# Quantizing the hidden activations of a dense layer: the multiply and rounding on ScalarE, the bound and the cast on VectorE

## The chip, the cores and the metric

One core of one Trainium2 chip runs the whole program. The metric is the device time of one launch in microseconds (us), the median over several launches. Engines are named as the profile names them: PE is TensorE (PEld its weight loads), DVE is VectorE, ACT is ScalarE, POOL is GpSimd, and SP is the engine whose queue issues most of the DMAs.

## What is computed

The input is 4096 tokens of 512 values. The first half of the reference adds a pooled attention term and normalizes (`y` below), then runs a feed-forward layer whose operands are quantized to small integers; the second half (a causal convolution and a mixture of eight experts, two per token) follows it and is not touched. The part that matters:

```python
def activation_quant(x):
    scale = 127.0 / clip(max(abs(x), axis=-1), EPS, None)
    return clip(round(x * scale), -128, 127) / scale
def bitlinear(x, w):            # w is rounded to -1, 0, 1 times one scale
    xn = rmsnorm(x)
    return activation_quant(xn) @ weight_quant(w).T
h = silu(bitlinear(y, w1)) * bitlinear(y, w2)      # 2048 values per token
x = x + bitlinear(h, w3)
```

The integers -128 to 127 are exact in bf16, so the three products run as bf16 matmuls and the scales are applied behind them.

## The kernel before

The dense layer takes the 4096 tokens in 32 tiles of 128, one token per partition. Every engine has an instruction stream of its own, written by hand, and all five streams are generated by one loop, `pipeline`, over stages s; in one stage the streams work on different tiles, and semaphores tie them together. An engine executes its stream strictly in order, and so does the SP queue: a wait holds up everything behind it.

In stage s:

- **PE** multiplies tile s with w1 and w2, each in two halves of 1024 columns: w1 half 0 (L1429), w2 half 0 (L1441), w1 half 1 (L1429), w2 half 1 (L1441), eight matmuls each; then the 16 matmuls of tile s-2 with w3 (`down`, L1452). The w1 products share one PSUM area, so each half of w1 waits for ACT's silu of the half before. The first half waits for the transposed tile `QyT` (semaphore `qyt_in`), `down` for the transposed halves `QT` (`qt_in`).
- **ACT** takes silu of half 0 (L812), casts the rounded y of tile s+1 to bf16 (L803, `cast_y`), casts half 0 of the rounded hidden tile s-1 from int16 to bf16 (L818, `cast_h`), takes silu of half 1, casts half 1 of tile s-1, and squares the halves of tile s for their mean (L826), with one square of y (L798) between.
- **DVE** adds the output of tile s-3 (L1093, `x1_add`), takes the statistics of tile s+3 and centres it (L1033, L1035, L1041), takes the largest y of tile s+2 (L1056), quantizes the hidden tile s-1 (L1085, `h_quant`: all 2048 columns times the scale, bounded by 127, written as int16), multiplies half 0 of tile s with its silu and takes its largest value (L1071, L1077), finishes the norm of tile s+3 (L1048), does the same two steps for half 1, and quantizes y of tile s+2 (L1063, `y_quant`).
- **POOL** works out the scale of hidden tile s-1 (`h_scales`, L667 to L677, the last of which signals `hq_done`), the scales of y (L624 to L660), and adds the attention term to tile s+4 (L618).
- **SP** issues, in this order: the transposing DMA of y of tile s+1 (L450, `turn_y`), the store of an output tile (L424), the two transposing DMAs of hidden tile s-1 (L458, `turn_h`, one per half; each waits for its half of `qh_done`), and then loads and fills for later: the attention rows every second stage (`PJ`, L420), a piece of the convolution's taps and a small fill of the scratch (stages 6 to 21, L482 and L473), an input tile (`XR`, stages 7 to 26, L432), and the convolution's input in four DMAs (`XW`, stages 4 to 19, L440 and L442). Behind them comes `turn_y` of the next stage.

`Ih` (int16) and `Qh` (bf16) are one place in SBUF with two names, single-buffered; `QT` and `H` are double-buffered. The part of SP's stream that sets the order:

```python
if tile(s + 1):
    turn_y(s + 1)
if tile(s - 3):
    store_x1(s - 3)
if tile(s - 1):
    turn_h(s - 1, 0)
    turn_h(s - 1, 1)
if s % TB == 0 and TB < (s + 6) // TB < B:
    load_pj((s + 6) // TB)
```

In stage 32, the first without a new tile for PE, SP first issues 16 DMAs of XW (it waits for the last w2 products), then `turn_h` of tile 31. PE there runs `down(30)`, a first piece of the convolution (L1480), and `down(31)`.

Of the kernel before, what the change touches and what calls it, by code (L numbers as in the profile page):

```python
# [20 lines left out]
ALU = mybir.AluOpType  # L21
ACT = mybir.ActivationFunctionType
# [5 lines left out]
QMAX = 127.0  # L28
# [4 lines left out]
def adaln_ffn_moe(nc, x, cond, taps, rms_w, WkT, WoT, gamma, beta, w1T, w2T, w3T, Wr, We, be, out):  # L33
    B, S, D = x.shape
    FF = w1T.shape[1]
# [36 lines left out]
    with ctx:  # L72
        def sem(name):
            return ctx.enter_context(nc.semaphore(name))
# [13 lines left out]
        def place(name, at, shape, dt=F32):  # L88
            n = 4 if dt in (F32, F32R) else 2
            size = n  # L90
            for s in shape[1:]:
                size *= s
            assert at >= 0 and at + size // 4 <= words, (name, at, size, words)
            return nc.alloc_sbuf_tensor_at(name, list(shape), dt, offset=base + 4 * at)
# [14 lines left out]
        H = [place(f"H{i}", a_h + FF * i, [P, FF]) for i in range(2)]  # L109
        a = a_h + 2 * FF  # L110
        Ih = place("Ih", a, [P, FF], I16)
        Qh = place("Qh", a, [P, FF], BF16)
# [50 lines left out]
        def col(i):  # L163
            return [sm[:, 2 * i + t:2 * i + t + 1] for t in range(2)]

        YMS, YR, YM, YB, YI, YQ, OG = (col(i) for i in range(7))
        HR, HM, HB, HI, HQ, RSTD = (col(8 + i) for i in range(6))
# [11 lines left out]
        NH = 2  # L179
# [118 lines left out]
        qt_in = [[sem(f"qt_in{h}{t}") for t in range(2)] for h in range(2)]  # L298
        pool_a = sem("pool_a")
        g_done, u_done, silu_done, hm_done = (sem(n) for n in ("g_done", "u_done", "silu_done", "hm_done"))  # L300
        hsq_done, hq_done = sem("hsq_done"), sem("hq_done")
        pool_h = sem("pool_h")
        hmc_done = sem("hmc_done")
        hint_done, qh_done, down_done, x1_done = (sem(n) for n in ("hint_done", "qh_done", "down_done", "x1_done"))
# [28 lines left out]
        def tile(n):  # L333

            return 0 <= n < NT
# [427 lines left out]
        def _(act):  # L763
# [28 lines left out]
            def square_y(n):  # L792
                act.wait_ge(y_done, n + 1)
                if n:
                    act.wait_ge(ysq_done, n)
                if n >= 2:
                    act.wait_ge(yq_done, n - 1)
                nc.scalar.activation(JUNK, Y[n % 3][:], ACT.Square, scale=D ** -0.5,  # L798
                                     accum_out=YMS[n % 2]).then_inc(ysq_done, 1)

            def cast_y(n):
                act.wait_ge(yint_done, n + 1)
                nc.scalar.copy(Qy[n % 2][:], Iy[n % 2][:]).then_inc(yqt_done, 1)  # L803

            def silu(n, c):
                p = NH * n + c
                act.wait_ge(g_done, p + 1)
                if c == 0:
                    act.wait_ge(og_done, n + 1)
                if n:  # L810
                    act.wait_ge(hsq_done, p - 1)
                nc.scalar.activation(SG[c][:], GP.rearrange("p a c -> p (a c)"), ACT.Silu, scale=OG[n % 2]).then_inc(silu_done, 1)  # L812

            def cast_h(n, h):

                half = slice(FF // 2 * h, FF // 2 * h + FF // 2)
                act.wait_ge(hint_done, n + 1)
                nc.scalar.copy(Qh[:, half], Ih[:, half]).then_inc(qh_done, 1)  # L818

            def square_h(n, c):  # L820

                half = slice(FF // 2 * c, FF // 2 * c + FF // 2)
                act.wait_ge(hm_done, NH * n + c + 1)
                if n >= 2:
                    act.wait_ge(hq_done, n - 1)
                nc.scalar.activation(SG[c][:], H[n % 2][:, half], ACT.Square, scale=FF ** -0.5,  # L826
                                     accum_out=(HSB if c else HSA)[n % 2]).then_inc(hsq_done, 1)

            def halo(j):

                act.wait_ge(x1_done, KEEP)
                rows = XW[QD * j:QD * j + OB].rearrange("p (b c) i -> p b c i", c=CB)[:, 0:B // 2, 0, :]
                none = IDF[QD * j:QD * j + OB, :].rearrange("p (o i) -> p o i", o=1).broadcast_to([OB, B // 2, NI])
                nc.scalar.activation(rows, none, ACT.Copy, scale=0.0).then_inc(halo_done, 1)

            def stage(s):
                if s <= 0:
                    return
                if tile(s):
                    silu(s, 0)  # L840
                if s == 1:
                    square_y(3)
                elif tile(s + 1):
                    cast_y(s + 1)
                if tile(s - 1):
                    cast_h(s - 1, 0)
                if tile(s):
                    silu(s, 1)
                if tile(s - 1):
                    cast_h(s - 1, 1)  # L850
                if tile(s):
                    square_h(s, 0)
                if tile(s + 3):
                    square_y(s + 3)
                if tile(s):
                    square_h(s, 1)
                if 0 <= s - KEEP - 4 < NQ:
                    halo(s - KEEP - 4)
# [13 lines left out]
            square_h(0, 0)  # L872
            square_h(0, 1)
            pipeline(stage)


# [68 lines left out]
        def _(dve):  # L945
# [81 lines left out]
            def stats(n):  # L1027
                t = n % 2
                if n < TB:
                    dve.wait_ge(add_sum, n + 1)  # L1030
                else:
                    dve.wait_ge(sum_done, n + 1 - TB)
                nc.vector.bn_stats(BS[t], Y[n % 3][:]).then_inc(stats_done, 1)  # L1033
                dve.wait_ge(stats_done, n + 1)
                nc.vector.bn_aggr(MV[t], BS[t]).then_inc(mv_done, 1)  # L1035

            def center(n):
                t = n % 2
                dve.wait_ge(norm_in, 32)
                dve.wait_ge(mv_done, n + 1)  # L1040
                nc.vector.scalar_tensor_tensor(out=Y[n % 3][:], in0=Y[n % 3][:], scalar=MV[t][:, 0:1], in1=GAM[:],  # L1041
                                               op0=ALU.subtract, op1=ALU.mult).then_inc(gam_done, 1)
# [8 lines left out]
            def y_max(n):  # L1051
                t = n % 2
                dve.wait_ge(y_done, n + 1)
                if n >= 2:
                    dve.wait_ge(yq_done, n - 1)
                nc.vector.tensor_reduce(YM[t], Y[n % 3][:], AX.X, ALU.max, apply_absolute_value=True).then_inc(ymax_done, 1)  # L1056
# [17 lines left out]
            def h_max(n, c):  # L1074
                half = slice(FF // 2 * c, FF // 2 * c + FF // 2)
                dve.wait_ge(hm_done, NH * n + c + 1)
                nc.vector.tensor_reduce(HMC[n % 2][:, c:c + 1], H[n % 2][:, half], AX.X, ALU.max,  # L1077
                                        apply_absolute_value=True).then_inc(hmc_done, 1)

            def h_quant(n):  # L1080
                dve.wait_ge(hq_done, n + 1)
                if n:
                    for h in range(2):
                        dve.wait_ge(qt_in[h][(n - 1) % 2], 16 * ((n - 1) // 2 + 1))
                nc.vector.tensor_scalar(Ih[:], H[n % 2][:], HQ[n % 2], QMAX, ALU.mult, ALU.min).then_inc(hint_done, 1)  # L1085

            def x1_add(n):
                t = n % 2
                dve.wait_ge(down_done, n + 1)
                dve.wait_ge(od_done, n + 1)  # L1090
                if n >= 2:
                    dve.wait_ge(x1_out[t], 16 * (n // 2))
                nc.vector.scalar_tensor_tensor(out=X1[t][:], in0=DN, scalar=OD[n % 3], in1=xt(n),  # L1093
                                               op0=ALU.mult, op1=ALU.add).then_inc(x1_done, 1)
# [3 lines left out]
            def stage(s):  # L1098
                if s <= 0:
                    return  # L1100
                if tile(s - 3):
                    x1_add(s - 3)
                if tile(s + 3):
                    stats(s + 3)
                    center(s + 3)
                if tile(s + 2):
                    y_max(s + 2)
                if tile(s - 1):
                    h_quant(s - 1)
                if tile(s):  # L1110
                    h_mul(s, 0)
                    h_max(s, 0)
                for w, c in WORK.get(s, ()):
                    ternary(w, c)
                if tile(s + 3):
                    norm(s + 3)
                if tile(s):
                    h_mul(s, 1)
                    h_max(s, 1)
                if tile(s + 2):  # L1120
                    y_quant(s + 2)
                if s in (NT, NT + 1):
                    spread(s - NT)
# [150 lines left out]
            for q in range(NK // CC):  # L1274
                h = q % 2
# [338 lines left out]
```

## Time and profile before

| | us |
|---|---|
| median of 3 runs | 845.53 (844.99 to 846.36) |
| the profiled execution, its own time | 845.81 |
| its span, first to last instruction | 844.1 |
| PE busy | 740.7 (88%) |
| DVE busy | 564.4 (67%) |
| POOL busy | 477.3 (57%) |
| ACT busy | 396.8 (47%) |

The dense layer's pipeline fills most of the stretch from about 70 to 432 us of the span. The rows in the section after next come from the trace of this execution. A row of the timeline has the start, the duration, the engine, the line and what it writes and reads; xN means that N like instructions in a row are shown as one, from the start of the first to the end of the last; the bracket is the idle time before and what ended it. SPq is the issue of a DMA by SP. A DMA's landing is the time from its issue to its semaphore. All numbers of a row that is a group are totals and means.

### The profile page before, as it was taken

Reading aid. Unit: us, or ns where it says so; the run is one execution under the profiler, and the core shown is the slowest. Engines: PE = TensorE matmul, PEld = TensorE weight load, DVE = VectorE, ACT = ScalarE, POOL = GpSimd, SP = SyncE. Lnnn points to the kernel's source line nnn. Section 1 sums busy time; section 2 is a strip of 40 time slices with the busy share of each in tenths; the row PEclk is TensorE's granted clock in tenths of the full one; section 3 lists DMA queues with packets and bytes.
Section 4 is the critical chain, followed back from the end, with each engine's and each line's share of the span. In section 5 each row is a group of like instructions: output and inputs, shape, how many; then the busy total and the mean of one; then the engine's idle time right before and its main releaser. Section 6 shows DMA issues by size and latency. Waiting matters only on the chain.

```text
span 844.1 us, 12610 instructions
## 1 busy us (share of the span) xinstructions
PE 740.7 (88%) x3913; PEld 432.6 (51%) x3945; DVE 564.4 (67%) x831; ACT 396.8 (47%) x635; POOL 477.3 (57%) x738
## 2 busy tenths in 40 slices
PE   1745599999999999999989999657999999899994
PEld 0112244444444444444446653345788888778773
DVE  2469999999999999997734424397834654444442
ACT  2056466666768877776412524034322333333332
POOL 1037889888888888884200000003567766876864
PEclk9987899999999999999999999768999999999998
DMA  9984148899999985555698999986468778877876
GB/s 359 388 328 134 31 88 149 137 182 180 178 180 189 183 157 132 117 116 92 138 232 148 113 116 258 116 197 215 77 126 165 143 136 160 152 146 143 167 143 105
DMA packets 230270, 137.50 MB, mean 163 GB/s; under 512 B 162798, under 2 KB 195054, under 8 KB 229054
## 3 DMA queue, kind: packets, MB, share of 16 engines
q1 hardware_dynamic: 210094, 99.94, 59.0%
q0 software_dynamic: 15456, 36.47, 23.2%
q10 hardware_dynamic: 4656, 0.30, 0.5%
q8 instruction: 33, 0.54, 0.3%
q14 instruction: 31, 0.25, 0.1%
HBM read 80.27 MB, written 35.42 MB: 137 GB/s over the span
## 4 chain that ended last, share of the span: by engine, by line
PE 45%; DMA 13%; POOL 11%; DVE 11%; issue 9%; SPq 6%; ACT 4%; POOLq 0%; DVEq 0%; ACTq 0%
DMA out_x<-YS,IDS 8%; PE PS L1480 8%; PE PS L1452 7%; PE PS L1572 7%; PE PS L1429 7%; PE PS L1441 7%; PE PS L1507 4%; POOL out_x L751 3%; SPq L381 2%; POOL ZR L742 2%; DVE Ih L1085 2%; PE PS L1529 1%; DMA QyT<-Qy 1%; ACT Qh L818 1%; DMA QT<-Qh 1%
## 5 line engine op out<-in xcount | busy, mean ns | idle before, releaser
L1572 PE MATMUL PS<-W,ZH 128*128 x552 | 179.5, 406 | 8.2 <-DVE ZL L1339 6.1
L742 POOL DMA_INDIRECT ZR<-z_scratch,IDG x69 | 69.6, 1008 | 156.1 <-DVE IDS L1303 135.4
L1429 PE MATMUL PS<-W,QyT 128*128 128x512 bf16 x502 | 123.0, 387 | 26.8 <-DMA QyT<-Qy 15.2
L751 POOL DMA_INDIRECT out_x<-YS,IDS x69 | 110.8, 1606 | 59.1 <-SPq L560 29.7
L939 ACT ACTIVATE YS<-YS,SG 128x512 f32<-128x512 f32 x69 | 50.0, 724 | 159.9 <-DVE YS L1357 159.9
L1441 PE MATMUL PS<-W,QyT 128*128 128x512 bf16 x504 | 120.9, 381 | 0.4
L1452 PE MATMUL PS<-W,QT 128*128 128x512 bf16 x498 | 116.4, 383 | 4.4 <-DMA QT<-Qh 2.9
L1572 PEld LDWEIGHTS PS<-W,ZH 128*128 128x128 f32 x552 | 100.4, 191 | 29.7 <-issue 11.5
L1572 PE MATMUL PS<-W,ZL 128*128 x276 | 109.6, 397 | 0.0
L1339 DVE TENSOR_TENSOR ZL<-PS,ZH 128x512 fp32r<-128x512 f32 x69 | 47.7, 691 | 78.2 <-ACT ZH L928 78.2
L1429 PEld LDWEIGHTS PS<-W,QyT 128*128 128x128 bf16 x512 | 49.7, 99 | 90.0 <-DMA QyT<-Qy 17.3
L812 ACT ACTIVATE SG<-PS,sm 128x1024 f32<-128x1024 f32 x64 | 71.0, 1109 | 45.5 <-PE PS L1429 45.5
L818 ACT CAST Qh<-Ih 128x1024 bf16<-128x1024 int16 x64 | 66.4, 1040 | 52.5 <-DVE Ih L1085 52.5
L1452 PEld LDWEIGHTS PS<-W,QT 128*128 128x128 bf16 x512 | 50.4, 99 | 65.7 <-issue 5.5
L1441 PEld LDWEIGHTS PS<-W,QyT 128*128 128x128 bf16 x512 | 50.4, 98 | 61.5 <-issue 2.1
L1071 DVE TENSOR_TENSOR H<-SG,PS 128x1024 f32<-128x1024 f32 x64 | 77.7, 1214 | 3.4 <-PE PS L1441 3.1
L1357 DVE TENSOR_TENSOR YS<-PS,BEB 128x512 f32<-128x512 f32 x69 | 47.6, 690 | 48.0 <-DMA out_x<-YS,IDS 26.0
L1077 DVE TENSOR_REDUCE sm<-H 128x1 f32<-128x1024 f32 x64 | 78.1, 1220 | 2.2
L1480 PE MATMUL PS<-XW,BD 128*64 128x128 f32 x512 | 74.2, 477 | 0.3 <-DVE BD L1135 0.3
L826 ACT ACTIVATE SG<-H 128x1024 f32<-128x1024 f32 x64 | 67.2, 1050 | 0.7 <-DVE H L1071 0.7
L1480 PEld LDWEIGHTS PS<-XW,BD 128*64 128x64 f32 x512 | 47.9, 165 | 26.4 <-issue 1.2
L1572 PEld LDWEIGHTS PS<-W,ZL 128*128 128x128 f32 x276 | 52.4, 190 | 11.7
(217 smaller groups left out, 1059.8 us busy)
## 6 DMA issues: line engine op xcount, KB each, us to landing
XW<-out_x SPq DMA_DIRECT2D x64, 240.0 KB, 4.5
X<-in_x SPq DMA_DIRECT2D x32, 256.0 KB, 10.0
out_x<-X SPq DMA_DIRECT2D x32, 256.0 KB, 3.6
z_scratch<-ZZ SPq DMA_DIRECT2D x8, 1024.0 KB, 24.1
WRAW<-in_We SPq DMA_DIRECT2D x8, 1024.0 KB, 12.6
XR<-in_x SPq DMA_DIRECT2D x20, 256.0 KB, 4.1
stage<-in_w1T SPq DMA_DIRECT2D x4, 1024.0 KB, 8.0
stage<-in_w2T SPq DMA_DIRECT2D x4, 1024.0 KB, 11.9
```

Source lines behind the costliest of these rows:

```text
L742: pool.indirect_dma_start(ZR[m % UZ][:], None, z_d, bass.IndirectOffsetOnAxis(IDG[:, m:m + 1].bitcast(U32), 0)) \
L751: pool.indirect_dma_start(x1_d, bass.IndirectOffsetOnAxis(IDS[:, m:m + 1].bitcast(U32), 0), YS[m % UN][:], None, compute_op=ALU.add).then_ ...
L812: nc.scalar.activation(SG[c][:], GP.rearrange("p a c -> p (a c)"), ACT.Silu, scale=OG[n % 2]).then_inc(silu_done, 1)
L818: nc.scalar.copy(Qh[:, half], Ih[:, half]).then_inc(qh_done, 1)
L826: nc.scalar.activation(SG[c][:], H[n % 2][:, half], ACT.Square, scale=FF ** -0.5, accum_out=(HSB if c else HSA)[n % 2]).then_inc(hsq_done, 1)
L1071: nc.vector.tensor_tensor(H[n % 2][:, half], SG[c][:], UP[c].rearrange("p a c -> p (a c)"), ALU.mult) \
L1077: nc.vector.tensor_reduce(HMC[n % 2][:, c:c + 1], H[n % 2][:, half], AX.X, ALU.max, apply_absolute_value=True).then_inc(hmc_done, 1)
L1429: i = nc.tensor.matmul(GP[:, a, :], QyT[t][:, k, :], W12[:, k, o:o + CH], start=(k == 0), stop=(k == KD - 1))
L1441: i = nc.tensor.matmul(UP[c][:, a, :], QyT[t][:, k, :], W12[:, k, o:o + CH], start=(k == 0), stop=(k == KD - 1))
L1452: i = nc.tensor.matmul(DN, QT[t][:, k, :], W3[:, k, :], start=(k == 0), stop=(k == KF - 1))
L1480: i = nc.tensor.matmul(PS[P // 2 * u:P // 2 * u + P // 2, b % 8, HB2 * (q % 4):HB2 * (q % 4) + HB2], BD[c % 2][:, u, q, :], XW[:, HB2 * h: ...
L1572: x = nc.tensor.matmul(bank[i], zz[i % 2][:, k, :], W2[:, bass.ds(q, 1), part, k, :].rearrange("p o d -> p (o d)"), start=(k == 0 and n == ...
```

## The change

The hidden tile's quantization is cut at another place. ScalarE now multiplies by the scale and rounds to int16, reading H, in two halves (`quant_h`), where it had cast int16 to bf16. VectorE, which had multiplied, bounded and rounded all 2048 columns at once, now bounds by 127 and casts int16 to bf16 in place, in two halves (`cast_h`). Each half is placed in VectorE's stream behind the product and the maximum of the same half of tile s; `turn_h` on SP waits for `qh_done` as before, which VectorE now signals.

```diff
-            def cast_h(n, h):
+            def quant_h(n, h):
                 half = slice(FF // 2 * h, FF // 2 * h + FF // 2)
-                act.wait_ge(hint_done, n + 1)
-                nc.scalar.copy(Qh[:, half], Ih[:, half]).then_inc(qh_done, 1)
+                act.wait_ge(hq_done, n + 1)
+                if n:
+                    act.wait_ge(qt_in[h][(n - 1) % 2], 16 * ((n - 1) // 2 + 1))
+                nc.scalar.activation(Ih[:, half], H[n % 2][:, half], ACT.Copy, scale=HQ[n % 2]).then_inc(hint_done, 1)
...
                 if tile(s - 1):
-                    cast_h(s - 1, 0)
+                    quant_h(s - 1, 0)
                 if tile(s):
                     silu(s, 1)
                 if tile(s - 1):
-                    cast_h(s - 1, 1)
+                    quant_h(s - 1, 1)
...
-            def h_quant(n):
-                dve.wait_ge(hq_done, n + 1)
-                if n:
-                    for h in range(2):
-                        dve.wait_ge(qt_in[h][(n - 1) % 2], 16 * ((n - 1) // 2 + 1))
-                nc.vector.tensor_scalar(Ih[:], H[n % 2][:], HQ[n % 2], QMAX, ALU.mult, ALU.min).then_inc(hint_done, 1)
+            def cast_h(n, h):
+                half = slice(FF // 2 * h, FF // 2 * h + FF // 2)
+                dve.wait_ge(hint_done, NH * n + h + 1)
+                nc.vector.tensor_scalar(Qh[:, half], Ih[:, half], QMAX, None, ALU.min).then_inc(qh_done, 1)
...
                 if tile(s + 2):
                     y_max(s + 2)
-                if tile(s - 1):
-                    h_quant(s - 1)
                 if tile(s):
                     h_mul(s, 0)
                     h_max(s, 0)
+                if tile(s - 1):
+                    cast_h(s - 1, 0)
                 for w, c in WORK.get(s, ()):
                     ternary(w, c)
                 if tile(s + 3):
                     norm(s + 3)
                 if tile(s):
                     h_mul(s, 1)
                     h_max(s, 1)
+                if tile(s - 1):
+                    cast_h(s - 1, 1)
                 if tile(s + 2):
                     y_quant(s + 2)
```

## Rows read from the trace of the kernel before

**Rows 1.** Busy time (x instructions), granted clock, DMA share in one stretch of the layer.

```profile
core 0: us, PE busy (x) PEld busy (x) DVE busy (x) ACT busy (x) POOL busy (x), PEclk, DMA share, GB/s
300.00:400.00 100.00, 99.53 (x456) 45.34 (x464) 90.95 (x109) 69.19 (x102) 78.93 (x165) 1.00 0.56 118
```

**Rows 2.** Timeline, PEld: the first weight loads of tiles 6, 8, 20 and 22.

```profile
141.08 0.96 PEld L1429 LDWEIGHTS PS<-W,QyT 128*128 128x128 bf16 x5
...
163.16 0.77 PEld L1429 LDWEIGHTS PS<-W,QyT 128*128 128x128 bf16 x5 [0.31 <-DMA QyT<-Qy]
...
289.58 0.31 PEld L1429 LDWEIGHTS PS<-W,QyT 128*128 128x128 bf16 x2
...
310.30 0.75 PEld L1429 LDWEIGHTS PS<-W,QyT 128*128 128x128 bf16 x4
```

**Rows 3.** Chain that ended last, stages 10 and 16: start, duration, what.

```profile
193.59 1.48 SPq L458
...
201.04 5.46 DMA QyT<-Qy
...
256.57 1.71 SPq L458
...
263.85 5.17 DMA QyT<-Qy
```

**Rows 4.** Timeline of SP, stage 12, from the second hidden transposition to turn_y.

```profile
214.58 1.62 SPq L458 DMA_TRANSPOSE QT<-Qh  x1
...
218.04 1.88 SPq L432 DMA_DIRECT2D XR<-in_x  x1
...
222.01 2.46 SPq L450 DMA_TRANSPOSE QyT<-Qy  x1
```

**Rows 5.** Tile QyT, 155 to 290 us: who waited (us, times), and landings.

```profile
  PEld PS L1429: 4.1, 6
...
DMA to landing us min/median/max: 3.9/4.9/5.5
```

**Rows 6.** Groups: what is removed, and the rows nearest to what is added.

```profile
L812 ACT ACTIVATE SG<-PS,sm 128x1024 f32<-128x1024 f32 x64 | 71.0, 1109 | 45.5 <-PE PS L1429 45.5
L818 ACT CAST Qh<-Ih 128x1024 bf16<-128x1024 int16 x64 | 66.4, 1040 | 52.5 <-DVE Ih L1085 52.5
L1085 DVE TENSOR_SCALAR Ih<-H,sm 128x2048 int16<-128x2048 f32 x32 | 41.0, 1282 | 8.0 <-POOL sm L677 7.6 <-DMA QT<-Qh 0.3
...
L979 DVE TENSOR_SCALAR W<-TMP x12: 694/694/716, 26.7 to 98.6; 128x2048 bf16<-128x2048 int16 x12
```

**Rows 7.** Timeline, stage 31 and the start of 32: the hand-over to SP and the tail.

```profile
403.54 1.61 PEld L1429 LDWEIGHTS PS<-W,QyT 128*128 128x128 bf16 x8
...
408.16 4.29 SPq L458 DMA_TRANSPOSE QT<-Qh  x2
...
410.15 1.03 ACT L818 CAST Qh<-Ih 128x1024 bf16<-128x1024 int16 x1
...
410.86 1.22 DVE L1071 TENSOR_TENSOR H<-SG,PS 128x1024 f32<-128x1024 f32 x1 [0.98 <-PE PS L1441]
...
412.12 1.22 DVE L1077 TENSOR_REDUCE sm<-H 128x1 f32<-128x1024 f32 x1
...
421.10 4.18 SPq L458 DMA_TRANSPOSE QT<-Qh  x2
...
426.72 5.08 PE L1452 MATMUL PS<-W,QT 128*128 128x512 bf16 x15 [2.86 <-DMA QT<-Qh]
```

**Rows 8.** Timeline, stage 22: the scale from POOL, and the cast of y.

```profile
312.86 0.41 POOL L677 TENSOR_SCALAR sm<-sm 128x1 f32<-128x1 f32 x1
...
313.45 0.61 ACT L803 CAST Qy<-Iy 128x512 bf16<-128x512 int16 x1
```

**Rows 9.** Timeline, PE waiting for silu at the two halves of tile 2.

```profile
95.13 3.57 PE L1429 MATMUL PS<-W,QyT 128*128 128x512 bf16 x8 [6.46 <-ACT SG L812]
...
103.28 1.04 PE L1429 MATMUL PS<-W,QyT 128*128 128x512 bf16 x4 [2.55 <-ACT SG L812]
```

## The prediction

> **What bounds the kernel now.** I read the busy times by stretch first. Between 300 and 400 us PE is busy for 99.5 of 100 us at full granted clock, DVE for 91, ACT for 69 [rows 1]: there PE is the bound, and work taken from DVE buys nothing by itself. The pace is read from the first weight loads of the tiles: tile 20 at 289.58, tile 22 at 310.30, so 20.72 us for two tiles, 10.36 for one [rows 2]. At that pace tiles 6 to 20 would take 14 x 10.36 = 145.0 us; they take 289.58 - 141.08 = 148.5 [rows 2]. So PE also loses 3.5 us, in stages 6 to 20, and the next question is to whom.
>
> The chain of waits answers: in these stages it runs through the SP queue. After the second transposition of a hidden tile SP issues taps, fill, input tile and four XW loads back to back and only then `turn_y`, whose landing PE is waiting for: 193.59 to 201.04 is 7.45 us of issuing, and the landing takes 5.46 more [rows 3]. Stage 16 has 7.28 and 5.17 [rows 3], stage 12 has 222.01 - 214.58 = 7.43 [rows 4]. These are even stages, which also load the attention rows; I take 7.3 for the six even stages from 8 to 18. The landings there have a median of 4.9 us, and weight loads waited for them 6 times, 4.1 us in all [rows 5]. What the reader is to see: SP has no reserve in these stages, and `turn_y` lands just when PE wants it.
>
> **What DVE and ACT gain and lose.** Removed on DVE: one operation of 1.28 us per stage [rows 6]. Added: two operations on 1024 columns, int16 to bf16. The nearest row is the bound of the weights, the same two types on 2048 columns, 0.694 us [rows 6]; half the columns cost between 0.35 and 0.69, and I take 0.45, since the fixed part stays. So DVE is relieved of 1.28 - 0.90 = 0.4 us a stage, 32 times, some 12 us of busy time. In place is not what that row shows; were such an operation to run at one column per cycle it would cost the 1.22 us of the maximum over 1024 columns [rows 7], the far end. On ACT 1.04 per half goes and an activation with a scale from memory comes: nearest is the silu with such a scale, 1.109 [rows 6]. I take 1.11, so 0.14 us a stage more, which ACT's idle 31% covers [rows 1]; without that cover it would be 4.5 us over 32 stages.
>
> Two new waits need a look. ACT now waits for POOL's scale in front of the silu of half 1, and behind that silu is PE's next w1 product. In stage 22 the scale is there at 313.27 and the cast of y that stands ahead ends at 314.06 [rows 8]: 0.8 us of cover. ACT also waits for the landing of the transpositions two stages back, which DVE waited for before and which cost it 0.3 us in all [rows 6]. I cost both at nothing; if the cover were gone, each microsecond of lateness would be one on PE. DVE waits for ACT's rounding: half 0 is ready some 5 us after the tile's first weight load and DVE comes to it after 6 us or more, so nothing there either.
>
> **What the hand-over to SP loses.** This is the large term. Now the second half of the hidden tile is ready when ACT's cast ends, 410.15 + 1.03 = 411.18, or 7.64 us after that tile's first weight load at 403.54 [rows 7]. In the changed order it is ready when DVE has done the product of half 1 of the new tile, its maximum, and the cast. The product cannot begin before PE's fourth group of eight: it started at 410.86, having waited 0.98 us for PE, and the maximum ends at 413.34 [rows 7]. With 0.45 for the cast, SP gets its signal at 413.75 or so, 10.2 us after the first weight load: 2.55 us later than now. Everything that SP has behind it moves too: store order, taps, fill, input tile, XW and `turn_y` of the next tile.
>
> That closes a loop. `turn_y` of tile s lands, PE starts tile s, 10.2 us later SP may issue the second transposition, 7.3 us later `turn_y` of tile s + 2 is issued, and it lands 4.9 to 5.1 us later. Together 10.2 + 7.3 + 5.0 = 22.5 us for two tiles, where PE needs 20.72. Bounds: with 7.0 and 4.6 it is 21.8; with 7.5 and 5.5 it is 23.2.
>
> From tile 8 to tile 20 there are six such pairs: 6 x 22.5 = 135.0 us, against 289.58 - 163.16 = 126.4 now [rows 2]: **8.6 us lost**. From tile 6 to 8 the kernel now needs 22.1 us [rows 2], part of it because POOL clears two buffers there and its scale is late; the change takes 1.28 us out of the loop from scale to ACT, and SP has a light stage, so I expect PE's 20.7 and **1.3 us gained**. Outside these stages SP idles and a hand-over 2.55 us later is covered by that.
>
> **Start and end of the layer.** At tile 2 PE waits 6.46 and 2.55 us for silu [rows 9]. The second of these silus follows a square of tile 1, whose product DVE does after `h_quant`; of its 1.28 us 0.45 comes back for the cast that now stands ahead: **0.85 us gained**. In stage 32 SP issues 16 XW loads before the last hidden transpositions (421.10), and PE waits 2.86 us for them before it goes on at 426.72 [rows 7]. Those 16 follow the transposition of stage 31, so they and all behind them come 2.55 us later: **2.5 us lost**. The convolution's first piece, which PE does before that wait, is delayed by 1.5 us at most, since its spread waits for the last cast, and hides in it.
>
> Sum: +8.6 - 1.3 - 0.85 + 2.5 = +8.9 us. The profiled execution took 845.8 us, 0.3 above the median of 845.5, so its time becomes 854.7; I leave the 0.3 in it.
>
> **A rule weighed.** The trace has SP issuing for 7.3 of every 10.4 us behind one signal, with PE waiting for what comes last [rows 3 to 5]. The Trainium skill (DMA: Bandwidth & Descriptors, Issuing engines are not separate DMA queues) says that issuing from several engines saves only the sequencer's time to initiate a DMA, usually small relative to the DMA itself. By that rule a late signal would cost next to nothing, and the result would be that of the first rival. The rows speak against it here.
>
> **Rivals.**
>
> *SP's time shrinks when it starts later.* The input tile's issue takes 1.88 us in stage 12 and `turn_y` 2.46 [rows 4], each longer than such issues elsewhere; if that is a queue that was full, an SP that has idled 2 us finds it empty. It decides from 1.8 us a pair: then 22.5 falls to 20.7 and PE runs at its pace. Tiles 6 to 20 take 145.0 (3.5 gained), the start gains 0.85, the tail loses 2.5: 845.8 - 1.8 = 844.0, faster, or 844 to 847 if it is not quite enough. Against it: the long issues stand right behind four others of the same stage, and these follow in the new order as well. Chance 0.19, of it 0.11 faster and 0.08 same.
>
> *It shrinks in part*, by about 1 us a pair: six pairs give back 6, so 849. Chance 0.12.
>
> *The cast in place is slow on DVE.* DVE works some 10.0 us a stage now: 9.4 of busy time for 10.36 [rows 1] and short gaps, which I put at 0.6. At 1.22 us a cast it becomes 10.0 - 1.28 + 2.44 = 11.2, past PE's 10.36, and the hand-over comes another 0.8 later: 0.8 us over some 16 stages and 1.2 over the SP-bound ones, 12 + 14 + 2.5, about 873. Against it is the row of the same types [rows 6]. Chance 0.04.
>
> **How the numbers follow.** The forecast (SP's loop paces stages 8 to 20) has 0.65; its own range by the bounds above is 6 x 21.8 to 6 x 23.2, so 850 to 859. A measurement of this kernel can tell about 0.2%, 1.7 us. Slower: 0.65 + 0.12 + 0.04 = 0.81; same 0.08; faster 0.11. The range runs from 846 (it takes in the partial case and the worst of the first rival) to 860.
>
> **What would show it.** In the changed kernel's trace: first weight loads of tiles 8 and 20 some 135 us apart, with PE waiting for QyT at every other tile; the second L458 of a stage 10.2 us behind the tile's first weight load; SP idle before it; casts of 0.4 to 0.5 us; DVE busy 12 us less; the last transpositions issued about 12 us later than now in all. I would be wrong if tiles 8 to 20 took under 128 us, which would say that SP's time or the landings shrank, or if PE waited for silu there, which would put the wait on ACT instead.

## The result and the profile after

| | kernel before | changed kernel |
|---|---|---|
| median | 845.26 (844.88 to 846.36, 4 runs) | 852.54 (852.1 to 854.16, 4 runs) |
| ratio, 95% interval | | 1.0084 [1.0068, 1.0101] |
| span of the profiled execution | 844.1 | 850.6 |
| PE, DVE, ACT, POOL busy | 740.7, 564.4, 396.8, 477.3 | 741.8, 552.8, 403.4, 456.0 |

The change costs 0.84%, some 7 us. It does what it says: VectorE (DVE) has 11.6 us less to do, ScalarE (ACT) 6.6 more. The page's costliest groups give what the two parts cost now (total and mean ns, then idle time before them and what ended it); for DVE's part the answer on its one line has the spread:

```profile
L820 ACT ACTIVATE Ih<-H,sm 128x1024 int16<-128x1024 f32 x64 | 73.0, 1143 | 6.2 <-POOL sm L677 6.2
```

```profile
L1086 DVE TENSOR_SCALAR Qh<-Ih x64: 416/418/1395, 94.2 to 422.7; 128x1024 bf16<-128x1024 int16 x64
```

The reader is to see that neither is the trouble: the cast in place takes 0.42 us at the median, the rounding 1.14, and the removed pair took 1.28 and twice 1.04 [rows 6]. So the time went elsewhere, and the first weight loads of the tiles (their starts) say where. In the changed kernel's timeline, PEld, tiles 6, 8, 16, 20 and 31 (the bracket is the idle time before and what ended it):

```profile
142.51 1.41 PEld L1432 LDWEIGHTS PS<-W,QyT 128*128 128x128 bf16 x8 [0.58 <-DMA QyT<-Qy]
...
163.75 1.19 PEld L1432 LDWEIGHTS PS<-W,QyT 128*128 128x128 bf16 x7 [0.85 <-DMA QyT<-Qy]
...
250.30 1.41 PEld L1432 LDWEIGHTS PS<-W,QyT 128*128 128x128 bf16 x8 [1.90 <-DMA QyT<-Qy]
...
293.95 0.98 PEld L1432 LDWEIGHTS PS<-W,QyT 128*128 128x128 bf16 x6 [1.40 <-DMA QyT<-Qy]
...
407.71 1.61 PEld L1432 LDWEIGHTS PS<-W,QyT 128*128 128x128 bf16 x8
```

Tiles 8 to 20 take 293.95 - 163.75 = 130.20 us where they took 126.42 [rows 2]: 3.8 lost. Tiles 6 to 8 take 21.24 instead of 22.08: 0.8 gained. From tile 20 to tile 31 both kernels run at PE's pace (113.8 and 114.0). The same reading for every kernel of this study, each from its own trace, is in this table; "tail" is from tile 31's first weight load to the last w3 weight load, "1 to 3" and so on are tiles:

| kernel | 1 to 3 | 3 to 6 | 6 to 8 | 8 to 20 | tail | span |
|---|---|---|---|---|---|---|
| before | 28.41 | 31.10 | 22.09 | 126.42 | 27.67 | 844.1 |
| changed | 29.25 | 31.54 | 21.25 | 130.19 | 30.24 | 850.6 |
| x1_wait_alone | 28.42 | 31.81 | 24.14 | 131.98 | 29.96 | 855.5 |
| x2_cast_before_max | 29.14 | 31.16 | 22.17 | 129.04 | 27.63 | 851.2 |
| x3_sp_order_new | 28.91 | 31.08 | 20.72 | 124.32 | 29.92 | 843.7 |
| x4_sp_order_old | 28.43 | 31.11 | 21.93 | 135.31 | 28.86 | 858.6 |
| x5_fills_on_act | 30.33 | 31.08 | 20.72 | 128.14 | 30.51 | 865.3 |
| x6_tile0_old_form | 29.48 | 32.16 | 21.61 | 134.10 | 31.43 | 873.0 |
| x7_order_and_tail | 29.24 | 31.08 | 20.72 | 125.97 | 24.82 | 857.4 |
| x9_tail_on_old | 28.41 | 31.22 | 22.25 | 130.00 | 23.29 | 857.1 |
| x10_change_again | 29.09 | 31.08 | 20.72 | 129.88 | 30.97 | 852.6 |
| x7b_order_and_tail | 30.06 | 31.08 | 20.72 | 124.32 | 25.00 | 840.9 |
| x8_order_tail_tile0 | 30.12 | 31.08 | 20.72 | 124.32 | 24.82 | 838.1 |

Changed against before, the stretches add up: +0.84 + 0.44 - 0.84 + 3.77 - 0.20 (tiles 20 to 31) + 2.57 = +6.6, and the span is 6.5 longer.

Each row is one execution, and the rows come from several chips (named under the experiments), so columns must be compared with care. x9 runs the same code as the kernel before up to stage 32, and its tiles 8 to 20 took 130.00 us on its chip, not 126.42. x7 and x7b are one program and differ by 1.65 there. The loss in this stretch is of one size where a pair from one chip can be read: 3.8 in the first comparison (126.42 to 130.19), 4.1 on the chip of x5 to x9 (x9 to x6, 130.00 to 134.10; x6 is the changed kernel but for tile 0).

Who makes PE wait in tiles 8 to 20? The answer on the tile QyT from 155 to 295 us (who waited, total and times, then issue to landing):

```profile
  PEld PS L1432: 9.4, 10
  PE PS L1432: 5.3, 7
...
DMA to landing us min/median/max: 2.8/5.0/5.3
```

The weight loads waited 9.4 us for the transposed y, where they had waited 4.1 [rows 5]. And the chain that ended last runs through SP at the even stages, as before [rows 3] (start, duration, what; stages 10 and 16; 14 and 18 repeat them):

```profile
195.21 1.23 SPq L458
...
202.38 4.36 DMA QyT<-Qy
...
260.26 1.23 SPq L458
...
266.89 5.21 DMA QyT<-Qy
```

Stage 16 can be read whole: tile 16's first weight load is at 250.30, SP issues the second hidden transposition at 260.26, 9.96 us later, and `turn_y` at 266.89, 6.63 later. Tile 18 starts when that lands. Stage 12 is the odd one. SP's timeline there:

```profile
213.87 4.11 SPq L458 DMA_TRANSPOSE QT<-Qh  x2
218.33 0.35 SPq L420 DMA_DIRECT2D PJ<-proj_scratch  x1
218.81 0.37 SPq L482 DMA_DIRECT2D T<-taps_scratch  x1
219.23 1.56 SPq L473 DMA_DIRECT2D z_scratch<-BET  x1
220.84 0.85 SPq L432 DMA_DIRECT2D XR<-in_x  x1
221.79 1.32 SPq L440 DMA_DIRECT2D XW<-out_x  x1
...
224.73 1.21 SPq L450 DMA_TRANSPOSE QyT<-Qy  x1
```

Here two small issues took 1.56 and 1.32 us instead of the usual 0.56 and 0.38, so SP needed 7.98 us; the landing behind it took only 2.8, the shortest of all. Over the six even stages from 8 to 18 the loop of two tiles splits into the hand-over (tile's first weight load to the second hidden transposition), SP's issuing, and issue of `turn_y` to PE's start. The means were 8.61 + 7.26 + 5.20 = 21.07 us in the kernel before and are 9.96 + 7.13 + 4.61 = 21.70 now. So the hand-over comes 1.35 later here, not 2.5: in these stages the kernel before already handed over late (8.0 to 9.9 us after the first weight load). SP's issuing gives back 0.1 of this and the landing of `turn_y` 0.6, which leaves 0.63 a pair; six pairs make the 3.8 us.

The tail, from the changed kernel's timeline (answers to [rows 7]):

```profile
414.31 1.14 ACT L820 ACTIVATE Ih<-H,sm 128x1024 int16<-128x1024 f32 x1
414.41 4.69 SPq L458 DMA_TRANSPOSE QT<-Qh  x2
...
415.03 1.22 DVE L1073 TENSOR_TENSOR H<-SG,PS 128x1024 f32<-128x1024 f32 x1 [0.64 <-PE PS L1444]
416.29 1.22 DVE L1079 TENSOR_REDUCE sm<-H 128x1 f32<-128x1024 f32 x1
417.42 0.42 DVE L1086 TENSOR_SCALAR Qh<-Ih 128x1024 bf16<-128x1024 int16 x1
...
427.91 4.12 SPq L458 DMA_TRANSPOSE QT<-Qh  x2
...
433.46 1.13 PE L1455 MATMUL PS<-W,QT 128*128 128x512 bf16 x3 [3.88 <-DMA QT<-Qh]
```

ACT has rounded the second half at 415.45, but the cast stands behind the product and the maximum and ends at 417.84, 10.1 us after the tile's first weight load (407.71). The last transpositions start 20.20 us after it, 17.56 before (421.10 - 403.54 [rows 7]).

### The profile page after: what moved, and what is told of

Same layout as the page of the kernel before. It is cut to its first block, busy times and chain, and to the rows that moved or that the text cites. A ratio compares the mean times of both kernels' runs of the same rounds, so it can differ in the third digit from the quotient of the medians.

```text
span 850.6 us, 12673 instructions
## 1 busy us (share of the span) xinstructions
PE 741.8 (87%) x3913; PEld 435.5 (51%) x3945; DVE 552.8 (65%) x863; ACT 403.4 (47%) x635; POOL 456.0 (54%) x738
## 4 chain that ended last, share of the span: by engine, by line
PE 56%; DMA 11%; DVE 11%; SPq 9%; issue 7%; POOL 3%; ACT 2%; POOLq 0%; DVEq 0%; ACTq 0%
PE PS L1575 14%; PE PS L1432 10%; PE PS L1483 8%; PE PS L1444 8%; PE PS L1455 7%; DMA QyT<-Qy 5%; PE PS L1510 4%; DMA out_x<-YS,IDS 4%; SPq L381 2%; PE PS L1559 2%; POOL out_x L751 2%; DVE H L1073 2%; PE PS L1532 1%; SPq L440 1%; SPq L442 1%
## 5 line engine op out<-in xcount | busy, mean ns | idle before, releaser
L1432 PE MATMUL PS<-W,QyT 128*128 128x512 bf16 x502 | 124.7, 390 | 28.1 <-DMA QyT<-Qy 19.0
L1444 PE MATMUL PS<-W,QyT 128*128 128x512 bf16 x504 | 121.8, 383 | 0.4
L1575 PEld LDWEIGHTS PS<-W,ZH 128*128 128x128 f32 x552 | 101.0, 193 | 26.6 <-issue 8.3
L820 ACT ACTIVATE Ih<-H,sm 128x1024 int16<-128x1024 f32 x64 | 73.0, 1143 | 6.2 <-POOL sm L677 6.2
```

Of the source, the lines that this page charges most:

```text
L820: nc.scalar.activation(Ih[:, half], H[n % 2][:, half], ACT.Copy, scale=HQ[n % 2]).then_inc(hint_done, 1)
L1432: i = nc.tensor.matmul(GP[:, a, :], QyT[t][:, k, :], W12[:, k, o:o + CH], start=(k == 0), stop=(k == KD - 1))
L1444: i = nc.tensor.matmul(UP[c][:, a, :], QyT[t][:, k, :], W12[:, k, o:o + CH], start=(k == 0), stop=(k == KD - 1))
L1575: x = nc.tensor.matmul(bank[i], zz[i % 2][:, k, :], W2[:, bass.ds(q, 1), part, k, :].rearrange("p o d -> p (o d)"), start=(k == 0 and n == ...
```

## The experiments

The theory: what costs is when SP gets the second hidden half, and in tiles 8 to 20 that lateness turns into PE's through SP's issues. The rivals: that a slower ACT or DVE pays, or that the landings do, or that the loss belongs to the chip or to the start of the layer. Ratios are against the kernel before, timed on the same chip. x1 to x4 shared one chip, x5, x6, x7 and x9 a second one, on which the kernel before takes 865 us, and x10, x7b and x8 a third. The changed kernel as it is was run beside them only on the third. So on the chip of x1 to x4 the loss of the unedited change is not known; 1.0084 and 1.0116 come from other runs.

### The lateness alone

The kernel before, untouched but for one wait: SP's second hidden transposition also waits until DVE has the maximum of half 1 of the next tile.

```diff
                 sp.wait_ge(qh_done, NH * n + h + 1)
+                if h and n + 1 < NT:
+                    sp.wait_ge(hmc_done, NH * (n + 1) + 2)
```

> The kernel before, with one wait more: SP's second hidden transposition also waits for the maximum of half 1 of the next tile, so it is handed over at about 9.9 us after that tile's first weight load, where it was 7.7; ScalarE and VectorE do the same work as before. Theory (the late hand-over to SP is the loss): tiles 8 to 20 take 129 to 131 us where they took 126.4, the last w3 product begins some 2.3 us later, 850.5 to 852 in all, some 6 us above before. Rival (the loss is in the new operations of ScalarE and VectorE, or in ScalarE's new wait for the scale): within 1 us of before, about 845.5.

Measured: 858.72 against 848.82, ratio 1.0127 [1.0096, 1.0157]. No operation differs from the kernel before, and tiles 8 to 20 take 131.98 us, the tail 2.3 more: the late hand-over alone makes a loss as large as the change's, and larger. It is also more than I expected (some 10 us by the ratio, not 6). The answer on waits from 155 to 295 us:

```profile
PEld PS L1431 <- DMA QyT<-Qy: 12.0, 8, 3.0
...
DVE Ih L1087 <- DMA QT<-Qh: 5.4, 5, 2.1
```

The second row is something that the changed kernel has not: the old `h_quant` writes both halves of the single-buffered `Ih` at once and must wait for both transpositions of the tile before; when these are late, so is it. The kernel before had 0.3 us of this [rows 6]. So x1 holds a second cost of lateness that belongs to the old form, and its excess over the change's loss is no measure of the change.

### A part of the lateness given back

The changed kernel, with the cast of half 1 ahead of the maximum of half 1.

```diff
                     h_mul(s, 1)
-                    h_max(s, 1)
                 if tile(s - 1):
                     cast_h(s - 1, 1)
+                if tile(s):
+                    h_max(s, 1)
```

> The changed kernel with the cast of half 1 moved ahead of the maximum of half 1 on VectorE, so the hand-over comes 1.2 us earlier, at about 8.8 us. Theory: SP's loop of two tiles shrinks from 21.7 by up to 1.2 to PE's 20.7 or SP's own 20.9: tiles 8 to 20 in 124.5 to 126.5 where the changed kernel has 130.2, the tail 1.2 us better; 846.5 to 848.5 in all. Rival (new operations or waits elsewhere): 852 as the changed kernel.

Measured: 851.6, ratio 1.0042 [1.0022, 1.0062], half of the loss of the first comparison. The tail is back at 27.63, as before the change. Tiles 8 to 20 take 129.04, some 1.2 less than in the changed kernel and far from the 124.5 to 126.5 expected: in the paced even stages the hand-over came 9.66 us after the first weight load (mean) instead of 9.96, not at 8.8. The timeline of stage 16 (tile 16's first weight load is at 250.59) says why:

```profile
256.99 1.14 ACT L820 ACTIVATE Ih<-H,sm 128x1024 int16<-128x1024 f32 x1
257.71 1.22 DVE L1073 TENSOR_TENSOR H<-SG,PS 128x1024 f32<-128x1024 f32 x1
...
258.61 1.27 POOL L618 TENSOR_TENSOR Y<-XR,PJ 128x512 f32<-128x512 f32 x1
258.84 1.32 DVE L1086 TENSOR_SCALAR Qh<-Ih 128x1024 bf16<-128x1024 int16 x1
```

ACT's rounding is ready at 258.13 and the cast starts 1.2 us earlier than in the changed kernel, 8.26 us after the first weight load. But it takes 1.32 us instead of 0.42, because POOL's addition for y has just begun: the cast ends 0.28 us after it. In this trace 15 of the 64 casts take over 0.6 us (1.3 to 2.3), among them those of half 1 in all six even stages from 8 to 18. All 15 began while that addition was running; 13 ended 0.28 or 0.29 us after it, two after the POOL operation that followed. So the maximum was in the way in the tail, where POOL adds nothing, and in the others the earlier cast ran into POOL.

### The work behind the signal moved ahead of it

The changed kernel, where SP issues the attention rows, the taps, the fill and the input tile before the second hidden transposition. Only the four XW loads then stand between it and `turn_y`.

```diff
                     turn_h(s - 1, 0)
-                    turn_h(s - 1, 1)
+                    if not tile(s):
+                        turn_h(s - 1, 1)
...
                     load_xr(s + 5)
+                if tile(s - 1) and tile(s):
+                    turn_h(s - 1, 1)
```

> The changed kernel with another order on SP: in stages 1 to 31 the second hidden transposition comes behind the loads of attention rows, taps, fill and input tile and ahead of XW, so that SP does not idle in front of it. Theory: SP no longer waits; tiles 8 to 20 take SP's own work, 124.3 to 126; the tail stays 2.5 us late, the start 1.4 us late; 847 to 848.5. Rival (the landings and DMA engines are what is full, not SP's waiting): tiles 8 to 20 stay above 129, 851 or more.

Measured: 847.44, ratio 0.999 [0.997, 1.001]. Every tile from 3 on starts 10.36 us after the last, which is PE's own pace. SP's timeline in stage 12:

```profile
210.44 1.29 SPq L458 DMA_TRANSPOSE QT<-Qh  x1
...
213.80 1.73 SPq L432 DMA_DIRECT2D XR<-in_x  x1
215.63 1.25 SPq L458 DMA_TRANSPOSE QT<-Qh  x1
...
219.13 1.81 SPq L450 DMA_TRANSPOSE QyT<-Qy  x1
```

From the second transposition to `turn_y` it is now 3.5 us, and the latter is issued 4.4 us before PE starts tile 14 (223.53). The answer on QyT names neither PE nor PEld among those who waited. So with the lateness left in but little queued behind it, stages 8 to 20 lose nothing: 124.32 us, 2.1 less than the kernel before in the first comparison. What remains of the loss is the tail (+2.2) and the start (+0.5), and the gains in tiles 8 to 20 and 6 to 8 (2.1 and 1.4) cancel them.

### The same order without the change

The kernel before, with the same edit of SP's order.

> The kernel before with the same new order on SP, as control. Theory: SP hardly waited there, so little is to be had: tiles 8 to 20 in 124.3 to 126.4, 843.5 to 845.5 in all. Rival: the order is good or bad by itself, and shifts this kernel by as much as it shifts the changed one (5 us).

Measured: 858.67, ratio 1.0115 [1.0084, 1.0147]; a clear miss. Tiles 8 to 20 take 135.31 us, and tiles 20 to 31 another 2.4 more (116.31). The waits from 155 to 300 us:

```profile
DVE Ih L1088 <- DMA QT<-Qh: 14.3, 9, 2.9
PEld PS L1432 <- ACT SG L815: 12.9, 13, 1.9
...
PEld PS L1432 <- DMA QyT<-Qy: 2.9, 2, 1.8
```

The wait for QyT shrinks here too (2.9 us instead of 4.1), but another loop opens: the second transposition is issued later, `h_quant` waits for its landing, ACT's cast waits for `h_quant`, and behind the cast is the silu on which PE waits. The new form waits half by half, on ACT, and in x3 that wait came to 0.4 us in all. So the change's form is what makes this order of SP harmless: with it the order takes the change's loss away, on the old form it costs 1.2%.

### The issues taken off SP

The changed kernel, where taps and fills (32 DMAs) are issued from ACT's queue: in the diff the lines leave SP's stage and enter ACT's, behind its last square. One wait for an input is added ahead of a later step on DVE, which had got it through SP's order.

```diff
-                if 0 <= s - 6 < NQ * TP:
-                    load_T((s - 6) // TP, (s - 6) % TP)
-                    blank(s - 6)
...
+                if 0 <= s - 6 < NQ * TP:
+                    load_T((s - 6) // TP, (s - 6) % TP)
+                    blank(s - 6)
```

> The changed kernel with the taps pieces and the small fills (32 DMAs in stages 6 to 21) issued from ScalarE's queue at the end of its stage; nothing else moves. SP has 1.1 to 1.9 us less to issue per stage between the second hidden transposition and turn_y. Theory (SP's loop paces stages 8 to 20): the loop of two tiles falls from 21.7 to PE's 20.7, tiles 8 to 20 in 124.3 to 126 where the changed kernel has 130.2; some 5 us below the changed kernel, ratio to before 1.001 to 1.004. Rival (the DMA engines' queues are what is full; the same transfers from another queue change nothing): tiles 8 to 20 in 129 to 131.

Measured: 864.91 against 865.25, ratio 0.9993 [0.9977, 1.001]; tiles 8 to 20 take 128.14 us. From the second transposition to `turn_y` SP now needs 4.4 us in four of the six even stages, 4.9 in the mean, yet the answer on QyT still has PE waiting:

```profile
  PEld PS L1435: 5.7, 7
  PE PS L1435: 2.8, 3
...
DMA to landing us min/median/max: 3.7/6.2/7.5
```

The nearest neighbour on this chip is x6: 134.10 us in tiles 8 to 20, 7.3 us of issuing, and a median landing of 4.9. Against it 2.4 us of issuing went, and 1.3 us came back as a longer landing (6.2): six us less over the stretch, but my 124.3 to 126 was too low. The ratio says that this, too, undoes the loss. The Trainium skill (DMA: Bandwidth & Descriptors, Issuing engines are not separate DMA queues) has the saving from another issuing engine as the sequencer's time to initiate, usually small beside the DMA. This run bears on it: the loop saved 1.0 us of the 2.4, so no more than that time, but 2.4 us of issuing beside a landing of 5 us is not small.

### The tail

In stage 32 only 8 of the 16 XW loads go ahead of the last hidden transpositions; once with SP's new order and the change (x7), once on the kernel before (x9).

```diff
                     load_xw(B // 2)
-                    load_xw(B // 2 + 1)
...
                 if s == NT:
+                    load_xw(B // 2 + 1)
                     sp.wait_ge(yint_done, NT)
```

> The changed kernel with the SP order of the earlier run and, in stage 32, only 8 of the 16 XW loads ahead of the last two hidden transpositions, the other 8 behind them. Theory (the tail is SP's queue too): the last w3 product begins about when the first piece of the convolution ends, 3.5 to 5 us earlier than in the earlier run, relative to tile 31's first weight load (25.7 us there); ratio to before 0.992 to 0.996. Rival (the convolution's second half then waits for the XW loads that come later): the gain is given back before 540 us, ratio 0.998 to 1.001.

> The kernel before with only the new order of stage 32 on SP. Theory: the last w3 product begins some 3 us earlier and at full clock, 3 to 4.5 us saved, ratio 0.995 to 0.997. Rival (as above, given back in the convolution): 1.000.

Measured: x7 856.0, ratio 0.9893 [0.9867, 0.992], x9 860.77, 0.9945 [0.9921, 0.9969]; x7 better than the 0.992 to 0.996 expected, x9 at the edge of 0.995 to 0.997. The tail shrinks to 24.82 and 23.29 us. The convolution behind it gives back about 1.5 of that in both (71.5 and 71.2 us from the last w3 load to its end, 69.9 in the other kernels on that chip).

### The same versions on one more chip

> The changed kernel once more, beside the versions built on it, on one chip. If the loss belongs to the program and not to one chip: ratio to the kernel before 1.006 to 1.010, tiles 8 to 20 in 129 to 134 us, tiles 1 to 3 in 29.2 to 29.5 us with a second stretch of half clock near 102 to 106 us. If it was the chip: ratio 1.000.

> The version with SP's new order and the shorter tail once more, on the same chip as the changed kernel. Expected: ratio to the kernel before 0.987 to 0.992, that is some 1.8% under the changed kernel on the same chip: tiles 8 to 20 in 124.3 to 126 us (4 to 8 under the changed kernel), tile 31 to the last w3 tile some 3.7 us sooner. If its earlier result was the chip's, the ratio is 0.997 or more.

Measured: the changed kernel 855.3 against 846.2, ratio 1.0116 [1.0087, 1.0145]; the version with order and tail 842.71, ratio 0.996 [0.9943, 0.9978]. The loss is the program's, not one chip's, and slightly larger here than in the first comparison, above the 1.006 to 1.010 expected. The version that combines the change with SP's new order and the shorter tail beats both kernels: 0.4% under the kernel before, 1.5% under the changed one (842.71 / 855.3 = 0.985). Its advantage over the kernel before was 1.1% on the second chip and 0.4% here. Part of this difference can be read: on the second chip x9, which is the kernel before up to stage 32, took 130.00 us for tiles 8 to 20, 3.6 (0.4%) more than the kernel before in the first comparison, while the version with order and tail took about the same on both chips (125.97 and 124.32). The rest stays open. Expected was a ratio of 0.987 to 0.992, so that was too hopeful; against the changed kernel it is 1.5% instead of the expected 1.8%, with tiles 8 to 20 as forecast (124.32). Its timeline in the tail:

```profile
418.13 3.72 SPq L458 DMA_TRANSPOSE QT<-Qh  x2
419.10 4.79 PE L1486 MATMUL PS<-XW,BD 128*64 128x128 f32 x32 [1.85 <-DVE BD L1141]
...
424.23 3.40 PE L1458 MATMUL PS<-W,QT 128*128 128x512 bf16 x15 [0.33 <-issue]
```

PE goes from the convolution's first piece into w3 without a wait for the transposition, which had cost 2.86 [rows 7] and then 3.88 us.

### The start of the layer

In the changed kernel tiles 1 to 3 take 0.84 us longer, where I had forecast a gain. PE's timeline there: the matmuls behind the second wait for silu in the kernel before ([rows 9] has the first), then those behind the first and the second in the changed kernel:

```profile
103.28 1.90 PE L1429 MATMUL PS<-W,QyT 128*128 128x512 bf16 x8 [2.55 <-ACT SG L812]
```

```profile
93.64 3.57 PE L1432 MATMUL PS<-W,QyT 128*128 128x512 bf16 x8 [4.83 <-ACT SG L812]
...
102.57 3.49 PE L1432 MATMUL PS<-W,QyT 128*128 128x512 bf16 x8 [2.54 <-ACT SG L812]
```

PE resumes sooner at both places, by 1.49 and 0.71 us. But the eight matmuls behind the second wait then take 3.49 us instead of 1.90. Busy times by stretch, the kernel before and then the changed one (behind the five engines stands the granted clock, third from the end):

```profile
92.00:96.00 4.00, 0.87 (x3) 0.35 (x4) 3.97 (x4) 3.08 (x4) 3.54 (x6) 0.54 0.22 45
96.00:100.00 4.00, 4.00 (x13) 1.52 (x12) 3.90 (x6) 1.03 (x3) 3.92 (x5) 0.60 0.47 89
...
102.00:106.00 4.00, 2.72 (x13) 1.29 (x14) 3.24 (x7) 1.73 (x4) 3.22 (x8) 1.00 0.16 33
```

```profile
92.00:96.00 4.00, 2.37 (x6) 0.90 (x7) 3.93 (x5) 3.57 (x5) 3.54 (x7) 0.56 0.06 12
96.00:100.00 4.00, 4.00 (x11) 1.31 (x9) 3.93 (x5) 0.72 (x2) 3.92 (x4) 0.59 0.29 56
...
102.00:106.00 4.00, 3.43 (x9) 1.28 (x10) 3.83 (x7) 1.80 (x3) 3.47 (x9) 0.59 0.50 98
```

Both kernels work near half clock (1.2 of 2.4 GHz) after the first wait, granted 0.54 to 0.60. After the second, of the same 2.5 us, the kernel before runs at full clock (1.00) and the changed one falls to half once more (0.59). Two runs tried to take this stretch away by giving tile 0 alone its old form (DVE all at once, two casts on ACT), in the changed kernel (x6) and in the version with order and tail (x8). The core of both edits:

```diff
+            def h_quant_first():
+                dve.wait_ge(hq_done, 1)
+                nc.vector.tensor_scalar(Ih[:], H[0][:], HQ[0], QMAX, ALU.mult, ALU.min).then_inc(hint_done, 1)
...
-                if tile(s - 1):
+                if s == 1:
+                    cast_first(0)
+                elif tile(s - 1):
                     quant_h(s - 1, 0)
```

> The changed kernel with hidden tile 0 quantized as before (VectorE multiplies and bounds, ScalarE casts), all others in the new form. In the changed kernel PE's first wait at tile 2 ends earlier but the second finds the granted clock at half again, and tile 3 begins 29.25 us after tile 1, where before had 28.41. Theory (PE resumes at 93.6 and finishes at 99.7, and a second idle of 2.5 us then brings the clock down again): with the old form tile 3 begins 28.2 to 28.6 us after tile 1, no second stretch at half clock, 0.8 to 1.3 us below the changed kernel in the trace. Rival (it is VectorE's order that delays tile 3, whatever the clock): the same gain in wait, but the stretch at half clock stays.

> As the version with SP's new order and the shorter tail, and the hidden tile 0 alone quantized in the old form (VectorE all of it at once, ScalarE the two casts). The theory that the new form of tile 0 lets PE resume earlier, and that the second stretch of half clock after the next wait takes that back: no half clock near 102 to 106 us, tiles 1 to 3 in 28.4 to 28.6 us instead of 29.2, ratio 0.001 under that of the version without it. The rival, that a later norm of tile 4 takes the same time (as in the changed kernel with this edit, 29.48): ratio equal within 0.001, tiles 1 to 3 in 29.3 to 29.6.

Measured: x6 ratio 1.0068 [1.0042, 1.0094], x8 0.9945 [0.9921, 0.997], which its neighbour's 0.996 does not differ from by more than the intervals. The stretch from 102 to 106 us, x6 and then x8:

```profile
102.00:106.00 4.00, 0.81 (x4) 0.41 (x5) 3.83 (x6) 3.23 (x6) 1.57 (x4) 1.00 0.00 0
```

```profile
102.00:106.00 4.00, 2.00 (x6) 0.80 (x7) 3.86 (x7) 2.46 (x4) 2.61 (x5) 0.79 0.08 17
```

In x6 the second half-clock stretch is gone, but tiles 1 to 3 take 29.48, not less: a norm on DVE that stands ahead took 1.75 us instead of 0.75, and the second wait grew to 3.65. In x8 it is not gone (0.79), and tiles 1 to 3 take 30.12, as without the edit (30.06) and outside both of the ranges expected. So the theory that tile 0's new form is what costs here fell in x8. What holds over all thirteen traces is that tiles 1 to 3 take 28.4 us in the four kernels that keep the old form in every tile and 28.9 to 30.3 in the others; why the clock falls a second time in one and not in the other stays open.

## Why the prediction was right or wrong

I forecast 854.7 us, from 846 to 860, slower; it is 852.5. The sign, the place and the mechanism are as argued, and the late hand-over to SP was shown on its own (x1) and by its removal (x3). The sizes:

- **The hand-over, +2.55 us.** Right where I read it: it is 10.1 us after the first weight load in the tail and 10.16 in stage 22, where the kernel before had 7.64 and 7.68. But I took the 7.64 of stage 31 for the kernel as a whole. In the even stages from 8 to 18 it was 8.61 before and is 9.96 now, so only 1.35 later. The sum did not need that difference, since it goes from the absolute 10.2.
- **The loop of two tiles, 22.5 us, 8.6 in all.** Wrong in size: 130.2 / 6 = 21.7, and 3.8 lost. The step that failed is its sum: all three terms were a little high, 10.2 for 9.96, 7.3 for 7.13 and 5.0 for 4.6. On a margin of 1.8 us a pair, 0.8 of error is near half of the term. The lower bound that I had worked out, 21.8, was the better value. One of the six pairs was shorter (20.8, the others 21.5 to 22.7) because of the 2.8 us landing in stage 12. Issue and landing need not be separate prices: in that stage SP's issues were slow and the landing quick, and where issues were taken off SP (x5), the landings grew. A worked sum is safer when it takes the two together from one stage. What came out is near my second rival (it shrinks in part, by about 1 us a pair), though less by SP's own time, which hardly shrank (7.26 to 7.13), than by the landing (issue to PE's start 5.20 to 4.61).
- **Tiles 6 to 8, -1.3.** Right in sign: -0.84 in this trace, -1.37 (20.72) in the repeat x10.
- **The start, -0.85.** Wrong in sign, +0.84, and +0.44 more at tile 6, where QyT is late by 0.58 (the repeat x10 has 29.09 and 31.08, so this second part is not in every execution). The wait for the second silu did end earlier, by 0.71, or 0.85 counted from tile 1's first weight load. What failed is that I carried the PE time behind it over unchanged: eight matmuls took 3.49 instead of 1.90 us at half clock.
- **The tail, +2.5.** Right: +2.57, and x2 has it back (27.63).
- **Work on DVE and ACT.** Cast 0.42 for 0.45 where POOL's addition does not run, rounding 1.14 for 1.11, DVE 11.6 us less for some 12. The new wait of ACT for POOL's scale costs 6.2 us in three places, 2.95 of it in stage 32, where PE has other work; between tiles 20 and 31 nothing is lost, so the cover was there.

That the sum was near is in part luck, because errors of both signs met: it had 4.8 us too much in tiles 8 to 20, and too little in two places, by 0.5 from 6 to 8 and by 2.1 at the start (0.85 + 0.84 + 0.44). The point named as a refutation, tiles 8 to 20 under 128 us, did not occur, and PE waited there for QyT and not for silu.

## What to carry to other kernels

Moving work off a busy engine changes when its product is handed over, and that counts more than the work: here 0.4 us less a stage on DVE came with a hand-over 2.5 us later (1.35 in the stages that SP paces), to a queue that had 7 us of issues behind it and no reserve. Before such a move, list what the in-order queue has behind the signal, and put ahead of it whatever does not need the signal (x3). And try the order with both forms: the order that brings the changed kernel from 1.0084 (first comparison) to 0.999 (x3) costs the old one 1.2% (x4), since a buffer that is written whole must wait for its last reader and one written by halves waits for the reader of that half. And look at what the other engines do at the new place: in x2 the cast was moved 1.2 us ahead and lost 0.9 of it to an addition on POOL.

## What the runs showed of the hardware that was not expected

- An operation of POOL and a cast or quantization of DVE that overlap can hold each other up. In x2 all 15 long casts (1.3 to 2.3 us, 0.42 otherwise) began while POOL's 1.27 us addition was running. In the kernel before it is POOL that waits: its small operation that meets the 1.28 us quantization `h_quant` takes 1.52 us at the median instead of 0.56 (L626, 16 times) or 1.17 instead of 0.23 (L624, 12 times). In the changed kernel, without `h_quant`, their medians are 0.57 and 0.24. These two lines have 26.6 us less to do, and this is the larger part of why POOL's busy time fell by 21 us (477.3 to 456.0) although its stream is unchanged; another, L657, has 8.2 more. It cost PE nothing, which did not wait for POOL in either kernel's paced stages.
- In one stage a long stretch of issuing came with a short landing: 7.98 and 2.8 us in stage 12 of the changed kernel, where stage 16 has 6.63 and 5.2. Of the six other traces with SP's old order and all its loads, five show it in that stage (7.6 to 9.0 us, landing 3.1 to 4.3) and the kernel before does not (7.43 and 5.1). The other even stages show no clear link. With 32 DMAs moved to another issuing queue it was 4.4 us and a median of 6.2. Why is open.
- After a wait of 2.5 us PE may resume at full clock (1.00, eight matmuls in 1.90 us) or at half (0.59 over 4 us, 3.49 us), in kernels whose PE stream is the same. What decides it was not shown.
